# Layer 1 of a graph network on one core: a weight wait behind the transposes, a bias as one-row products, and an output norm read straight from PSUM

## What is computed

```
def _L1_mix_ref(x, norm_w, w_qkv, mem_kv, w_out, b_out, out_norm_w):
    def _rmsnorm_seq(x, w):
        n = jnp.sqrt(jnp.sum(x * x, axis=2, keepdims=True))
        return x / jnp.maximum(n, 1e-12) * w * jnp.asarray(DIM ** 0.5, x.dtype)
    xn = _rmsnorm_seq(x, norm_w)
    q, k, v = jnp.split(xn @ w_qkv, 3, axis=2)
    ...
    q = jax.nn.softmax(q, axis=-2) * scale
    k = jax.nn.softmax(k, axis=-1)
    context = jnp.einsum('bhdn,bhen->bhde', k, v)
    out = jnp.einsum('bhde,bhdn->bhen', context, q)
    ...
    out = out @ w_out + b_out
    return _rmsnorm_seq(out, out_norm_w)
```

## Time and profile before

| | |
|---|---|
| median of 3 runs | 3170.18 us (3159.96 to 3177.58) |
| profiled execution, its own time | 3178.86 us |
| its span | 3177.1 us |
| PE busy | 2755.8 us (87% of the span) |
| DVE / ACT / POOL busy | 1686.3 / 1069.7 / 1191.3 us |
| mean granted PE clock | 0.926 of full |

### The profile page before, as it was taken

How to read it: one execution, slowest core, us unless ns; L and a number is a source line. 1 busy time by engine, 2 the same in 40 slices (tenths; PEclk the granted TensorE clock), 3 DMA queues, 4 the chain that set the end, 5 groups by cost and what they waited for, 6 DMA issues and landing times. The chain is left out here.

```text
span 3177.1 us, 45609 instructions
## 1 busy us (share of the span) xinstructions
PE 2755.8 (87%) x16695; PEld 1759.6 (55%) x16695; DVE 1686.3 (53%) x3412; ACT 1069.7 (34%) x2449; POOL 1191.3 (37%) x1445
## 2 busy tenths in 40 slices
PE   8997989899999989989997975999789968859784
PEld 4654557565556756555554654777445645535552
DVE  8865577643556764366744554222246355552643
ACT  3243336422433642222323222444332315420132
POOL 2030677767367766852312222111003205500042
PEclk9998999899998999989998996999889969979897
DMA  2001345433035543440100004999811029720197
GB/s 63 1 27 48 116 149 153 146 93 123 31 116 153 158 130 95 128 116 31 44 14 27 27 20 154 417 417 416 308 26 35 31 100 317 256 79 1 33 374 259
DMA packets 164074, 415.57 MB, mean 131 GB/s; under 512 B 23939, under 2 KB 75683, under 8 KB 140372
## 3 DMA queue, kind: packets, MB, share of 16 engines
q1 hardware_dynamic: 149349, 362.36, 33.6%
q0 software_dynamic: 12960, 42.48, 3.5%
q10 hardware_dynamic: 1555, 7.95, 1.0%
HBM read 325.63 MB, written 87.09 MB: 130 GB/s over the span
## 5 line engine op out<-in xcount | busy, mean ns | idle before, releaser
L2649 POOL TENSOR_SCALAR raw<-raw 128x512 f32<-128x512 f32 x380 | 269.3, 709 | 1117.2 <-PE ps L496 317.2
L510 PE MATMUL ps<-units,ARENA 128*125 128x512 f16 x2160 | 474.1, 381 | 1.1 <-DVE ARENA L1843 0.6
L1790 DVE TENSOR_TENSOR ARENA<-tmp,ARENA 128x500 f16<-128x500 f32 (+3 forms) x289 | 208.1, 725 | 395.5 <-ACT ARENA L1347 215.9
L496 PE MATMUL ps<-ARENA,units 128*128 128x500 f16 (+1 forms) x2160 | 388.0, 342 | 2.0 <-DVE ARENA L2538 2.0
L510 PEld LDWEIGHTS ps<-units,ARENA 128*125 128x125 f16 x2160 | 290.7, 137 | 178.7 <-DVE X L2355 16.5
L496 PEld LDWEIGHTS ps<-ARENA,units 128*128 128x128 f16 x2160 | 211.1, 98 | 178.5 <-issue 6.5
L1346 ACT ACTIVATE tmp<-ps,cols 128x500 f32<-128x500 f32 (+1 forms) x204 | 129.7, 636 | 382.7 <-PE ps L496 329.6
L2653 POOL TENSOR_TENSOR AT<-raw,AT 128x512 f16<-128x512 f32 x200 | 238.4, 1192 | 17.0
L2653 POOL TENSOR_TENSOR units<-raw,units 128x512 f16<-128x512 f32 x180 | 220.7, 1226 | 15.3
L2697 POOL DMA_INDIRECT ARENA<-rows_d,proj x81 | 79.9, 987 | 365.2 <-DVE ARENA L2145 339.2
L2702 POOL DMA_INDIRECT picks_d<-ARENA,proj x81 | 82.0, 1013 | 346.6 <-DVE ARENA L2185 345.9
(11 more groups left out here) (451 smaller groups left out, 4818.5 us busy)
## 6 DMA issues: line engine op xcount, KB each, us to landing
ARENA<-split_d SPq DMA_DIRECT2D x135, 1024.0 KB
raw<-in_moe SPq DMA_DIRECT2D x200, 256.0 KB, 3.0
split_d<-AT SPq DMA_DIRECT2D x200, 256.0 KB, 2.5
raw<-in_units SPq DMA_DIRECT2D x180, 256.0 KB, 2.5
ARENA<-split_d SPq DMA_DIRECT2D x27, 1280.0 KB
rows_d<-ARENA SPq DMA_DIRECT2D x6, 896.0 KB
ARENA<-picks_d SPq DMA_DIRECT2D x6, 896.0 KB
ARENA<-picks_d ACTq DMA_DIRECT2D x6, 896.0 KB
```

The source lines that it names most:

```text
L496: ins = pe.matmul(o[:, 0:nt * R], wt, mv_, start=(i == 0), stop=(i == len(steps) - 1))
L510: ins = pe.matmul(o[0:R, :], th(srcT, h, k, t, 1), w(k, g), start=(i == 0), stop=(i == len(steps) - 1))
L1790: tt(lo, tmp[:, staged[0] % STAGES, 0:width], hi, ALU.subtract).then_inc(sem("lo_T"), s.one("lo_T"))
L2649: pool.tensor_scalar(r, r, WEIGHT_SCALE, 1.0, ALU.mult, ALU.mult).then_inc(sem("pool_step"), 1)
```

## The change

Three edits, all for layer 1 alone. (1) PE's wait for the query unit moves from ahead of the first transposes to ahead of the first products, and ACT and DVE take chunk 2's transposes earlier in their loops (ahead of tile 2 on ACT and ahead of tile 3 on DVE, where it was tile 4). (2) The bias is scaled and split into two float16 rows by DVE, behind the value evictions, and enters each output tile as two matmuls with one row of ones as weights, so a tile is 14 matmuls. (3) ACT squares out of PSUM as soon as a bank is filled, DVE waits for that and multiplies the bank by the weight row in its one eviction, and the norm is applied in the step that adds to X; `inverse_norms` carries the factor. The bias row's slot is given back before the context instead of in the output stage.

```
-                        ins = pe.matmul(o[0:R, :], th(srcT, h, k, t, 1), w[:, g, k, :], start=(i == 0), ...)
+                    if offset:
+                        for i, part in enumerate(offset):
+                            pe.matmul(o[0:R, :], out_ones, part, start=(i == 0), stop=False)
+                        ins = pe.matmul(o[0:R, :], th(srcT, h, k, t, 1), w[:, g, k, :], start=(i == 0 and not offset), ...)
...
-                pe.wait_ge(*loaded())
+                weights = loaded()
                 u, w = unit()
                 if mem:
-                    by_chunks(lambda c: transposed_chunk(...), lambda c: gemm_N_chunk("YT", w, "qsub", c), "lo_T")
+                    def queries_chunk(c):
+                        if c == 0:
+                            pe.wait_ge(*weights)
+                        gemm_N_chunk("YT", w, "qsub", c)
+
+                    by_chunks(lambda c: transposed_chunk(...), queries_chunk, "lo_T")
...
# ACT
-                    if mem and t == CH[1][0]:
+                    if mem and t == 2:
                         evac_pair("YT", "yT", scale=lambda k: col("L1nw", k), steps=chunk(2))
...
-                            act.wait_ge(sem("att_out"), s.more("att_out", 1))
-                            ins = act.activation(nat(M, t), nat(Y, t), ACT.Square, accum_out=small[0:R, 32 + t:33 + t])
+                            filled = marks["out_banks"] + t
+                            act.wait_ge(sem("filled_dve"), filled + 1)
+                            o = PS[RING["dve"][filled % len(RING["dve"])]]
+                            act.activation(nat(M, t), o[0:R, :], ACT.Square, scale=WS, accum_out=...).then_inc(sem("squared"), ...)
# DVE
-                    if mem and t == CH[1][0]:
+                    if mem and t == 3:
                         low_parts("YT", "yT", 2)
...
+                if mem:
+                    scaled_row = row_slots[0:1, ROWS.index("L1bout") % ROW_SLOTS, :]
+                    row("L1bout")
+                    dve.memset(out_ones, 1.0)
+                    ts(scaled_row, scaled_row, WEIGHT_SCALE, None, ALU.mult)...
+                    dve.tensor_copy(out_offset[0], scaled_row)...
+                    tt(out_offset[1], scaled_row, out_offset[0], ALU.subtract)...
+                    row_free("L1bout")
...
-                        stt(nat(Y, t), o[0:R, :], WS, b, ALU.mult, ALU.add).then_inc(sem("att_out"), ...)
+                        dve.wait_ge(sem("squared"), s.more("squared", 1))
+                        stt(nat(Y, t), o[0:R, :], WS, b, ALU.mult, ALU.mult).then_inc(sem("att_out"), ...)
...
-                    inverse_norms(*tiles)
-                    b = row("L1onw")
-                    for t in range(*tiles):
-                        stt(nat(Y, t), nat(Y, t), rstd[0:R, t:t + 1], b, ALU.mult, ALU.mult)...
+                    inverse_norms(*tiles, gain=float(D) ** 0.5)
                     for t in range(*tiles):
-                        stt(nat(X, t), nat(Y, t), float(D) ** 0.5, nat(X, t), ALU.mult, ALU.add)...
+                        stt(nat(X, t), nat(Y, t), rstd[0:R, t:t + 1], nat(X, t), ALU.mult, ALU.add)...
```

More of the change, by code:

```diff
@@ L244, in build @@
         bd = YT[:, 0:D]
+        out_offset = [YT[0:1, D + i * (D // 2):D + (i + 1) * (D // 2)].bitcast(F16) for i in range(2)]
+        out_ones = YT[0:1, 2 * D:2 * D + 64].bitcast(F16)[:, 0:R]
         split1_d = nc.dram_tensor("split1_d", (NE, 4, 128, 2 * KC * D), F16, kind="Internal").ap()
@@ L465, in gemm_T_chunk, with gemm_N_chunk @@
                     ins.then_inc(sem("filled_act"), 1)
-            def gemm_N_chunk(srcT, w, name, c):
+            def gemm_N_chunk(srcT, w, name, c, offset=None):
                 t0, nt = CH[c]
@@ L473, in gemm_N_chunk @@
                     o = bank("dve", name)
+                    if offset:
+                        for i, part in enumerate(offset):
+                            pe.matmul(o[0:R, :], out_ones, part, start=(i == 0), stop=False)
                     for i, (k, g, h) in enumerate(steps):
-                        ins = pe.matmul(o[0:R, :], th(srcT, h, k, t, 1), w[:, g, k, :], start=(i == 0), stop=(i == len(steps) - 1))
+                        ins = pe.matmul(o[0:R, :], th(srcT, h, k, t, 1), w[:, g, k, :], start=(i == 0 and not offset), stop=(i == len(steps) - 1))
                     ins.then_inc(sem("filled_dve"), 1)
@@ L1101, in linear_attention @@
                 mem = layer == 1
-                pe.wait_ge(*loaded())
+                weights = loaded()
                 u, w = unit()
                 if mem:
-                    by_chunks(lambda c: transposed_chunk(lambda t, a, b: nat(Y, t, a, b), "y", "yT", c),
-                              lambda c: gemm_N_chunk("YT", w, "qsub", c), "lo_T")
+                    def queries_chunk(c):
+                        if c == 0:
+                            pe.wait_ge(*weights)
+                        gemm_N_chunk("YT", w, "qsub", c)
+                    by_chunks(lambda c: transposed_chunk(lambda t, a, b: nat(Y, t, a, b), "y", "yT", c), queries_chunk, "lo_T")
                 else:
+                    pe.wait_ge(*weights)
                     gemm_N("YT", lambda k, g: w[:, g, k, :], "qsub")
@@ L1174, in linear_attention @@
                         heads_chunk(c)
+                    marks["out_banks"] = len(given["dve"])
                     for c in range(len(CH)):
                         pe.wait_ge(sem("lo_D"), s.more("lo_D", KC))
-                        gemm_N_chunk("K", w, "att_out", c)
+                        gemm_N_chunk("K", w, "att_out", c, out_offset)
                 else:
@@ L1662, in linear_attention @@
                         for t in range(t0, t0 + nt):
-                            act.wait_ge(sem("att_out"), s.more("att_out", 1))
-                            ins = act.activation(nat(M, t), nat(Y, t), ACT.Square, accum_out=small[0:R, 32 + t:33 + t])
-                        ins.then_inc(sem("act_step"), s.one("act_step"))
-                        act.wait_ge(*s.latest())
+                            filled = marks["out_banks"] + t
+                            act.wait_ge(sem("filled_dve"), filled + 1)
+                            o = PS[RING["dve"][filled % len(RING["dve"])]]
+                            act.activation(nat(M, t), o[0:R, :], ACT.Square, scale=WS, accum_out=small[0:R, 32 + t:33 + t]).then_inc(sem("squared"), s.one("squared"))
+                        act.wait_ge(sem("squared"), t0 + nt)
                         roots(nt, small[0:R, 32 + t0:32 + t0 + nt], 0.0, dst=std[0:R, t0:t0 + nt])
@@ L2435, in linear_attention @@
                     ts(nat(M, t), o[0:R, :], WS, None, ALU.mult).then_inc(sem("v2"), s.one("v2"))
+                if mem:
+                    scaled_row = row_slots[0:1, ROWS.index("L1bout") % ROW_SLOTS, :]
+                    row("L1bout")
+                    dve.memset(out_ones, 1.0)
+                    ts(scaled_row, scaled_row, WEIGHT_SCALE, None, ALU.mult).then_inc(sem("dve_step"), s.one("dve_step"))
+                    dve.wait_ge(*s.latest())
+                    dve.tensor_copy(out_offset[0], scaled_row).then_inc(sem("dve_step"), s.one("dve_step"))
+                    dve.wait_ge(*s.latest())
+                    tt(out_offset[1], scaled_row, out_offset[0], ALU.subtract).then_inc(sem("dve_step"), s.one("dve_step"))
+                    dve.wait_ge(*s.latest())
+                    row_free("L1bout")
                 dve.wait_ge(sem("kexp"), s.more("kexp", 1))
@@ L2457, in out_chunk @@
                         return
-                    b = row("L1bout")
+                    b = row("L1onw")
                     for t in range(*tiles):
@@ L2461, in out_chunk @@
                         o = s.bank("dve")
[L2462 to L2466, removed]
-                    inverse_norms(*tiles)
-                    b = row("L1onw")
-                    for t in range(*tiles):
-                        stt(nat(Y, t), nat(Y, t), rstd[0:R, t:t + 1], b, ALU.mult, ALU.mult).then_inc(sem("dve_step"), s.one("dve_step"))
+                        dve.wait_ge(sem("squared"), s.more("squared", 1))
+                        stt(nat(Y, t), o[0:R, :], WS, b, ALU.mult, ALU.mult).then_inc(sem("att_out"), s.one("att_out"))
                     dve.wait_ge(*s.latest())
@@ L2473, in out_chunk @@
                         row_free("L1onw")
+                    dve.wait_ge(sem("std"), s.more("std", 1))
+                    inverse_norms(*tiles, gain=float(D) ** 0.5)
                     for t in range(*tiles):
-                        stt(nat(X, t), nat(Y, t), float(D) ** 0.5, nat(X, t), ALU.mult, ALU.add).then_inc(sem("dve_step"), s.one("dve_step"))
+                        stt(nat(X, t), nat(Y, t), rstd[0:R, t:t + 1], nat(X, t), ALU.mult, ALU.add).then_inc(sem("dve_step"), s.one("dve_step"))
                     dve.wait_ge(*s.latest())
@@ L2485, in linear_attention, with inverse_norms @@
                     by_chunks(lambda c: low_direct("K", (KC * c, KC * c + KC)), out_chunk)
```

(4 more changed lines are left out.)

## The result

| | before | after |
|---|---|---|
| median | 3175.88 us (18 runs) | 3162.14 us (18 runs) |
| profiled execution, its span | 3177.1 us | 3160.3 us |

The ratio is 0.9954, 95% interval 0.9936 to 0.9971: 14.6 us less on 3176, with 9.2 and 20.3 as the ends of the interval. The forecast was a gain of 16.5 us (0.52%). At 0.46% the measurement stands just on the near side of the 0.5% line that the chances were drawn at. The time itself was forecast as 3153.7 us and is 3162.1, inside the range of 3143 to 3168; 5.7 of these 8.4 us come from the kernel before, whose median is 3175.88 over 18 runs and was 3170.18 over the three that the forecast stood on.

A forecast was written before the change was run, and what follows sets the result against it. Query stage bound by PE's weight wait, then DVE; output stage by DVE. Query edit 8.2 plus output edits 8.3 gave 16.5 us: profiled 3178.86 becomes 3162.4, and, 8.7 above the median, the forecast 3153.7 us, range 3143 to 3168.

The forecast's parts named there:

- Weights ready: Query stage: POOL's four converted quarters, 2.5 us for the first and 3.2 for each other, ready at 1723.0, bounds 1720.9 and 1724.2.
- Slow start: Query stage: the first 10 matmuls after the weight wait run at the lower clock, costing 2.1 us.
- DVE's first tile: Query stage: DVE starts tile 0 5.5 us earlier and tile 4 8.7 earlier; 0.5 lost beside POOL leaves 8.2.
- Offset matmuls: Output stage: one-row bias products cost 0.216 us each, bounds 0 and 0.425; eight before chunk 0's last eviction cost 1.7.
- Chunk 0: Output stage: earlier square saves 0.72 us, dropped norm pass 2.74; additions cost 0.24 more, bias products 1.7; sum -1.5.
- Chunk 1: Output stage: norm pass and eviction before square go, tile 7 restarts 0.8 us faster, additions avoid POOL (1.78); sum -5.8.
- Chunk 2 with the short operation held up: Output stage end: -1.9 us including the last layer norm partly clear of POOL, against 0.9 for a DVE operation behind POOL.
- the first rival: Query stage: POOL's conversion queues behind DVE's eight low parts, weights 5.4 us later, edit 1 gives 4.9; chance 0.15.
- ACT's squares late in chunk 1: Output stage, fifth rival: ACT's queue delays squares of tiles 4 to 6, 0.8 us per waiting tile, 5 us; chance 0.05.
- Clock that stays low: Query stage, slower case: PE's clock does not rise after the new start, 0.21 us lost per 512-wide product; chance 0.04.
- The second rival: Both restarts, query products and tile 7: PE's clock as before or better, gain 19.4 us, time 3150.8; chance 0.15.
- Gain not passed on: Later stages, third rival: transfers or PE's clock lose a third or more, 5 to 11 us gained, 3162; chance 0.15.

## Why the prediction was right, point by point

- **Weights ready at 12.1 us after the product, bounds 10.0 and 13.3.** 13.1, inside the bounds and just past the 11.5 to 13 us that were named as the sign of being right. The three disturbed quarters took 3.3 to 3.6, not 3.2. DVE was busy for 9.37 of these 10.46 us, not for little over half of them, since the low parts were stretched too (8.4 us for eight, where 8 x 0.68 is 5.4).
- **Slow start, 2.1 us.** 1.4 (48 products in 11.91 against 10.53). Low for some seven products and not ten.
- **DVE's first tile 5.5 us earlier, tile 4 8.7, end of stage 8.2.** 5.0, 8.4 and 8.1, counted from `bnT`'s end. The order of chunk 2 was 3.2 us of the 8.7. Tile 4 did come 3.4 us nearer to tile 0, and undoing the order showed 4.7, because the moved weight wait alone was worth less than its 5.0 at tile 0.
- **Offset matmuls, 0.216 each, 1.7 us in chunk 0.** This term was too small: 0.72 a tile, 2.9 us in chunk 0, above the sum's value and inside the bound of 0.425 a matmul. The prediction read the nine-row product of the earlier trace rows for its duration alone. The answer of the trace for that line goes on, in the kernel before:

```profile
  issue: 10.7, 28
```

  10.7 us of idle time ahead of the weight loads of 28 of those matmuls, 0.38 each, is the same 0.38 that stands at the one-row pair here. The Trainium skill, page "TensorEngine Tiling (Array Packing)", section "Key Properties", says that a change of the tiling mode drains the engine. The trace fits that: with full-height operands the 0.38 is gone and a tile takes 3.02. But the page gives no figure and does not say that a matmul of few rows is such a change, and no run here shows it either. What is shown is that the height of the operands is what costs.
- **DVE's split of the bias row hidden.** Right; it took 0.16 to 1.52 us an operation beside POOL, 2.7 us in all, and the wait behind it went from 8.71 to 5.58.
- **Chunk 0, -1.5 us.** -0.5 up to the end of its layer norm (24.24 against 24.76 from the first matmul), by the offset matmuls' 1.1.
- **Chunk 1, -5.8.** -5.2, and the near agreement is partly luck, as three terms were off. Tile 7 was filled in 3.41 us, at full clock in the profiled execution, where 3.9 were taken. The 0.72 for the eviction ahead of the square was not gained whole: DVE's eviction now waits for the square, and in this chunk no table load hides it, so from tile 7's fill to the clamp it is 1.51 us (1889.47 to 1890.98) against 1.78 before (1891.47 in the earlier trace rows to the row below), 0.27 less. And the layer norm beside POOL took 4.09, where the earlier trace rows had 3.33.

```profile
1893.25 0.17 DVE L2488 TENSOR_SCALAR std<-std 125x4 f32<-125x4 f32 x1 [1.09 <-ACT std L1405]
```

- **Chunk 2 with the short operation held up, -1.0.** -1.1. The clamp took 1.05 instead of 0.17, as foreseen. But the sum has in here 0.4 us that the last layer norm of four tiles was to gain by getting out of POOL's way; it lost 0.8 instead (4.09 against 3.33, counted in chunk 1), and the rest of chunk 2 did better than forecast (its additions took 1.88 us against 1.29, 0.6 longer and not 1.0).
- **The lock of the shared ports as the first rival, 15.4 us to the weights.** It did not happen in that measure: POOL lost 3.0 us, and so did DVE's eight low parts. Yet the mechanism is there. The clamp of two columns that took 1.05 us beside POOL and 0.17 without is a short instruction behind a long one of the other engine, and DVE's maximum out of PSUM took 0.69 in both cases. The Trainium skill, page "SBUF — State Buffer", section "Who interferes with whom", says just this of which instructions take part (`tensor_scalar` can contend, `tensor_reduce` on trn2 never does), and the trace agrees. It doesn't bear out that each blocks the other for its whole length: undisturbed, the eight low parts (5.4 us) and three quarters (7.5 us) come to 12.9 us, and they took 10.5.
- **ACT's squares late in chunk 1.** No: ACT was done with tile 4 before DVE came (its squares stand at 1883.0 to 1885.0 in the timeline, DVE's first eviction at 1885.31), a margin of about 1.6 us for tile 4 where 1.4 was forecast.
- **Clock that stays low.** No: some seven products, 2.6 us (1731.89 to 1734.47), were slow at the new start. The second rival, both restarts fast, came in by half in the profiled execution: tile 7 was fast, the query products' start was not. And the chance taken at tile 7 was a true one: three of six kernels with the same PE work in that stage had it slow.
- **Gain not passed on.** Not seen: the context stage took 28.24 and 28.33, and the ratio's 14.6 us stand beside 14.8 from the stages. But its interval begins at 9.2, so the loss of a third that this rival names isn't ruled out.
- **The chances.** They don't follow from the rivals. The first, third and fifth (0.35) and not quite half of the 0.46 for the sum (0.21) lie within 0.5%, 0.56 in all, which leaves 0.40 for faster; the text has 0.46 and 0.50. The measurement fell on the side that it held the less likely of the two.

The forecast's sum of 16.5 was 1.7 too high, nearly all in the output stage. The offset matmuls are 1.1 of it, the last layer norm 1.2 and the eviction in chunk 1 0.45; tile 7's clock, better than taken, and smaller terms gave 1.1 back. The mechanism held: both waits moved as forecast, and the terms named are sizes.

## What to carry to other kernels

A matmul with few rows among full ones is not priced by its duration: look at the idle time that the trace books to "issue" beside such a line, and try the same operand padded with zero rows, or several rows in one matmul. When a faster part ends in the same wait, see what the engine does at the restart: here the cheaper versions of the offset gained next to nothing in the stage until PE was kept busy through the wait. And where a stage waits for a conversion on POOL beside DVE work, ask when the converted data is really needed; holding it back was worth 3.5 us of the stage.

## What the runs showed of the hardware that was not expected

- Two matmuls with one row between full ones cost 0.715 us a tile where two full ones cost 0.43; the difference shows as 0.38 us of idle time ahead of the weight loads on each side.
- The same instruction stream with the same 1.78 us wait of PE was followed by twelve products in 2.80 us in three kernels and in 4.49 us in three. Longer waits: 2.63 us, 3.98; 3.28 us, 4.44 and 5.33; 3.93 us, slow as well. With 0.74 and 0.75 us of wait, behind extra matmuls, it was 2.75 both times. What decides between the levels isn't known.
- The part of the program ahead of the query stage, the same instructions in all kernels, took from 1703.5 to 1725.2 us in fourteen profiled executions. That spread is larger than the gain that was to be measured, and is why stages and not spans are compared here. 16 us of it are there at one early mark, POOL's first start on a unit after 600 us (643.0 to 659.4); its cause is not known.
